# Latent attention on one core: the swapped rotary halves by transfers within SBUF in place of a second projection, and their sum on POOL

## The reference, cut to what matters

```python
kv_c = kv @ W_kvc                                   # 64 wide
q_c = q @ W_dq                                      # 96 wide
q_nope = (q_c @ W_uq).reshape(b, lq, H, HD)         # HD = 128
q_rope = (q_c @ W_qr).reshape(b, lq, H, R)          # R = 64
k_nope, v = kv_c @ W_uk, kv_c @ W_uv
k_rope = kv_c @ W_kr                                # 64, the same for all heads
q_rope, k_rope = _rope(q_rope), _rope(k_rope)       # [x1*cos - x2*sin, x1*sin + x2*cos]
scores = (q_nope . k_nope + q_rope . k_rope) / sqrt(HD + R)
out = softmax(where(good, scores, NEG)) @ v @ W_o
```

## Time and profile before

| | |
|---|---|
| median of 3 runs | 2310.97 us (2307.03 to 2313.88) |
| the profiled execution, its own time | 2306.32 us |
| its span, first to last instruction | 2304.5 us |
| busy share of the span | PE 89%, DVE 69%, ACT 54%, POOL 13% |
| mean granted clock of TensorE | 0.952 |
| the attention's four groups | some 80 us each, from 1200 to 1520 us of the span |

### The profile page before, as it was taken

The page is one execution under the profiler, slowest core; times in us unless marked ns, Lnnn a source line. Parts: engine busy times, 40 slices in busy tenths (PEclk is TensorE's granted clock), DMA queues, the critical chain, the costliest instruction groups (busy, mean ns, idle before and its releaser), DMA issues. The chain is left out here.

```text
span 2304.5 us, 46693 instructions
## 1 busy us (share of the span) xinstructions
PE 2055.2 (89%) x18816; PEld 1569.9 (68%) x18816; DVE 1600.1 (69%) x2975; ACT 1238.0 (54%) x2456; POOL 302.9 (13%) x307
## 2 busy tenths in 40 slices
PE   7978989899899898888889998979889779999996
PEld 4654458677555787566656666768656658999996
DVE  5756657677465897888857877857566676766763
ACT  2325664545476444555546547655478524665653
POOL 0010000011310000010000000000100113444432
PEclk9979999999999999999989999999899879999998
DMA  3020010100100002000020000010200035667663
GB/s 121 22 66 23 14 44 1 37 1 1 60 20 25 11 1 73 1 1 1 1 81 1 9 18 0 0 37 1 73 2 2 15 112 185 211 194 222 195 208 89
DMA packets 59688, 125.70 MB, mean 55 GB/s; under 512 B 12968, under 2 KB 42281, under 8 KB 59337
## 3 DMA queue, kind: packets, MB, share of 16 engines
q1 hardware_dynamic: 50666, 110.96, 14.2%
q0 software_dynamic: 8832, 12.06, 2.5%
HBM read 108.79 MB, written 15.80 MB: 54 GB/s over the span
## 5 line engine op out<-in xcount | busy, mean ns | idle before, releaser
L268 PE MATMUL ps<-ffn_xh,ffn_wh 128*128 128x256 f32 x644 | 184.1, 286 | 1.5 <-DVE ffn_xl L4388 1.5
L268 PE MATMUL ps<-ffn_xh,ffn_wl 128*128 128x256 f32 x644 | 182.2, 283 | 0.0
L268 PE MATMUL ps<-ffn_xl,ffn_wh 128*128 128x256 f32 x644 | 182.1, 283 | 0.0
L4383 DVE TENSOR_TENSOR ffn_wl<-ffn_fresh,ffn_wh 128x1792 fp32r<-128x1792 f32 x69 | 139.4, 2023 | 26.5 <-ACT ffn_wh L4263 26.5
L216 POOL TENSOR_TENSOR all_rstd<-all_mv,all_cst 128x4 f32<-128x4 f32 x40 | 8.5, 212 | 1060.8 <-DVE all_mv L194 1060.8
L1981 DVE SCALAR_TENSOR_TENSOR attn_xc<-attn_cx,all_w,attn_xc 128x512 f32<-128x512 f32 (+1 forms) x144 | 107.0, 749 | 40.2 <-ACT attn_xc L1832 36.8
L4263 ACT ACTIVATE ffn_wh<-ffn_fresh 128x1792 fp32r<-128x1792 f32 x69 | 116.9, 1695 | 14.6 <-DMA ffn_fresh<-in_l3f_w 14.6
L268 PEld LDWEIGHTS ps<-ffn_xh,ffn_wh 128*128 128x128 f32 x644 | 123.4, 192 | 1.7 <-DVE ffn_xl L4388 1.7
L268 PEld LDWEIGHTS ps<-ffn_xl,ffn_wh 128*128 128x128 f32 x644 | 123.5, 192 | 0.0
L268 PEld LDWEIGHTS ps<-ffn_xh,ffn_wl 128*128 128x128 f32 x644 | 123.4, 192 | 0.0
L3037 ACT ACTIVATE xattn_sc<-xattn_sc,xattn_mx 128x128 f32<-128x128 f32 x256 | 98.8, 391 | 17.7 <-DVE xattn_mx L3135 17.7
(11 more groups left out here) (486 smaller groups left out, 6065.6 us busy)
## 6 DMA issues: line engine op xcount, KB each, us to landing
ffn_fresh<-in_l3f_w SPq DMA_DIRECT2D x69, 896.0 KB, 4.9
all_w<-in_ctxT SPq DMA_DIRECT2D x12, 512.0 KB, 5.6
all_w<-in_ctx SPq DMA_DIRECT2D x8, 512.0 KB, 6.9
all_x<-in_x_rows SPq DMA_DIRECT2D x4, 512.0 KB, 7.4
all_x<-x_seq SPq DMA_DIRECT2D x4, 512.0 KB, 5.4
all_w<-in_l2x_o SPq DMA_DIRECT2D x1, 2048.0 KB, 9.4
xattn_ctxT<-in_ctxT SPq DMA_DIRECT2D x4, 512.0 KB, 3.8
all_w<-in_l2f_up SPq DMA_DIRECT2D x1, 2048.0 KB, 11.3
```

Source lines behind the costliest of these rows:

```text
L268: last = pe.matmul(out, a, b, start=start and n == 0, stop=stop and n == 2)
L4383: dve.tensor_tensor(wl[:, j % 2, piece(q)], fresh[:, piece(q)], wh[:, j % 2, piece(q)].bitcast(F32), ALU.subtract).then_inc(low_ready.sem, 1)
```

## The change

The second rotary product is gone, with its weights (`SWAP`, half of `wkr`) and their preparation. ACT now copies each rotary product out of PSUM into half 0 of a `rot` buffer (there are 5 in place of 3, `nB`). SP then issues four transfers, each of 32 partitions and 512 values (64 KB), that write half 1 of the buffer with the halves of each head swapped. DVE multiplies half 0 by cos and half 1 by sin, in place and from SBUF. POOL adds the two into `kR` or `qR`. The transfers of tile n wait until DVE has multiplied tile n - 3, since tiles three apart share a semaphore. `dist`, a scratch tile of the mask, moves from `rot` to `sc`. In the diff some long lines are cut where nothing changes.

```diff
-    LAT, ROPE, SWAP = range(3)
-    wh = k.sb("wh", [MQ, 3, PAIRS, P], F32R)
-    wkr = k.sb("wkr", [ML, 2, 2, MR])
+    LAT, ROPE = range(2)
+    nB = 5
+    wh = k.sb("wh", [MQ, 2, PAIRS, P], F32R)
+    wkr = k.sb("wkr", [ML, 2, MR])
...
-    rot = arena[:, 0:6 * T].rearrange("p (b m t l) -> p b m t l", b=3, m=2, t=TG)
+    rot = arena[:, 0:2 * nB * T].rearrange("p (b m t l) -> p b m t l", b=nB, m=2, t=TG)
-    dist = rot[:, 0, 0]
+    dist = sc[:, 0, 0]
...
                 act.activation(by_head(wh, ROPE), raw[:, :, :], ACT.Copy).then_inc(rounded.sem, 1)
-                act.activation(by_head(wh, SWAP)[:, :, 0:half], raw[:, :, half:MR], ACT.Copy).then_inc(rounded.sem, 1)
-                act.activation(by_head(wh, SWAP)[:, :, half:MR], raw[:, :, 0:half], ACT.Copy).then_inc(rounded.sem, 1)
...
-                dve.wait_ge(*rounded(0, 3))
-                for a, b in ((slice(0, half), slice(half, MR)), (slice(half, MR), slice(0, half))):
-                    dve.tensor_tensor(by_head(wl, SWAP)[:, :, a], raw[:, :, b], by_head(wh, SWAP)[:, :, a].bitcast(F32), ALU.subtract)
...
+            def swap(i, n):
+                sp.wait_ge(*rot_copied(i, n + 1))
+                if n >= 3:
+                    sp.wait_ge(*rot_ready(i, n - 2))
+                a = rot[:, n % nB].rearrange("p m t l -> p m (t l)")
+                for e in range(2):
+                    for h in range(2):
+                        into = slice(e * MR + h * half, e * MR + (h + 1) * half)
+                        from_ = slice(e * MR + (1 - h) * half, e * MR + (2 - h) * half)
+                        sp.dma_start(a[into, 1], a[from_, 0]).then_inc(swapped[n % 3].sem, 16)
+
             with sp.Fori(0, GROUPS - 1) as i:
+                for n in range(1 + PAIRS):
+                    swap(i, n)
                 sp.wait_ge(*ctx_used(i, 1))
                 sp.dma_start(ctxT[:, :, :], src[i + 1]).then_inc(ctx_loaded.sem, 16)
+            for n in range(1 + PAIRS):
+                swap(last_group, n)
...
             with pool.Fori(0, GROUPS) as i:
+                for n in range(1 + PAIRS):
+                    pool.wait_ge(*rot_ready(i, n + 1))
+                    a = rot[:, n % nB].rearrange("p m t l -> p m (t l)")
+                    pool.tensor_tensor(kR[:, :] if n == 0 else qR[:, n - 1, :], a[:, 0], a[:, 1], ALU.add).then_inc(rope_ready.sem, 1)
                 norm.pool(pool, i + 1)
...
-                for p in range(PAIRS):
-                    act.wait_ge(*lat_psum(i, p + 1))
-                    act.activation(qL[:, p, :], TB[(p + 1) % 2][:, :], ACT.Copy).then_inc(lat_ready.sem, 1)
+                for n in range(1 + PAIRS):
+                    act.wait_ge(*rot_psum(i, n + 1))
+                    if n >= nB:
+                        act.wait_ge(*rope_ready(i, n - nB + 1))
+                    act.activation(rot[:, n % nB, 0].rearrange("p t l -> p (t l)"), S[n % 4][:, :], ACT.Copy).then_inc(rot_copied.sem, 1)
+                    if n >= 1:
+                        act.wait_ge(*lat_psum(i, n))
+                        act.activation(qL[:, n - 1, :], TB[n % 2][:, :], ACT.Copy).then_inc(lat_ready.sem, 1)
...
                 for n in range(1 + PAIRS):
-                    dve.wait_ge(*rot_psum(i, n + 1))
...
-                    if n >= 1:
-                        add_halves(n - 1)
-                add_halves(PAIRS)
+                    dve.wait_ge(*swapped[n % 3](i, 64 * (n // 3 + 1)))
+                    for half_of, by in enumerate(("cos", "sin")):
+                        a = rot[:, n % nB, half_of]
+                        last = dve.tensor_tensor(a, a, k.c[by].unsqueeze(1).broadcast_to([P, TG, P]), ALU.mult)
+                    last.then_inc(rot_ready.sem, 1)
...
                 for n in range(1, 1 + PAIRS):
-                    if n >= 2:
-                        pe.wait_ge(*rot_ready(i, n - 1))
-                    for s in range(2):
-                        at = (slice(None), ROPE + s, n - 1, slice(None))
-                        last = three(pe, S[2 * s + n % 2][:, :], (wh, wl), (qh, ql), at, slice(None), True, True)
-                    last.then_inc(rot_psum.sem, 1)
+                    if n >= 4:
+                        pe.wait_ge(*rot_copied(i, n - 3))
+                    three(pe, S[n % 4][:, :], (wh, wl), (qh, ql), (slice(None), ROPE, n - 1, slice(None)), slice(None), True,
+                          True).then_inc(rot_psum.sem, 1)
...
-                pe.wait_ge(*rot_ready(i, 1 + PAIRS))
+                pe.wait_ge(*rot_copied(i, 1 + PAIRS))
                 scores(0)
```

More of the change, by code:

```diff
@@ L2854, in phase_xattn2 @@
     kvx = k.sb("kvx", [P, TG, ML])
-    rot = arena[:, 0:6 * T].rearrange("p (b m t l) -> p b m t l", b=3, m=2, t=TG)
-    pT = arena[:, 6 * T:10 * T].rearrange("p (b e n) -> p b e n", b=2, e=2)
+    rot = arena[:, 0:2 * nB * T].rearrange("p (b m t l) -> p b m t l", b=nB, m=2, t=TG)
+    pT = arena[:, 2 * nB * T:(2 * nB + 4) * T].rearrange("p (b e n) -> p b e n", b=2, e=2)
     qL = k.sb("qL", [P, PAIRS, T])
@@ L2966, in _ @@
                     dve.tensor_copy(wkv[:, :, e, :], v["kvc"])
-                    for s in range(2):
-                        dve.tensor_copy(wkr[:, s, e, :], v["kr"][:, s, :])
+                    dve.tensor_copy(wkr[:, e, :], v["kr"][:, 0, :])
                 dve.wait_ge(*small(0, 32))
@@ L2981, in phase_xattn2 @@
     rot_psum = Signal(k, "rot_psum", 1 + PAIRS)
+    rot_copied = Signal(k, "rot_copied", 1 + PAIRS)
+    swapped = [Signal(k, f"rot_swapped{b}", 64 * (1 + PAIRS) // 3) for b in range(3)]
     rot_ready = Signal(k, "rot_ready", 1 + PAIRS)
@@ L3104, in _ @@
                 scale_ternary()
-                def add_halves(n):
-                    dve.wait_ge(*rot_ready(i, n + 1))
-                    a = rot[:, n % 3].rearrange("p m t l -> p m (t l)")
-                    out = kR[:, :] if n == 0 else qR[:, n - 1, :]
-                    dve.tensor_tensor(out, a[:, 0], a[:, 1], ALU.add).then_inc(rope_ready.sem, 1)
-                for n in range(1 + PAIRS):
-                    dve.wait_ge(*rot_psum(i, n + 1))
-                    if n >= 3:
-                        dve.wait_ge(*rope_ready(i, n - 2))
-                    a, b = (S[2 * s + n % 2][:, :].rearrange("p (t l) -> p t l", t=TG) for s in range(2))
-                    dve.tensor_tensor(rot[:, n % 3, 0], a, k.c["cos"].unsqueeze(1).broadcast_to([P, TG, P]), ALU.mult)
-                    dve.tensor_tensor(rot[:, n % 3, 1], b, k.c["sin"].unsqueeze(1).broadcast_to([P, TG, P]),
-                                      ALU.mult).then_inc(rot_ready.sem, 1)
-                    if n >= 1:
-                        add_halves(n - 1)
-                add_halves(PAIRS)
+                for n in range(1 + PAIRS):
+                    dve.wait_ge(*swapped[n % 3](i, 64 * (n // 3 + 1)))
[3 more added lines that the diff above has]
+                    last.then_inc(rot_ready.sem, 1)
                 def scale(n, e):
@@ L3191, in _ @@
                 pe.wait_ge(*latent_ready(i, 1))
-                for s in range(2):
-                    last = pe.matmul(S[2 * s][:, :], wkr[:, s].rearrange("p e r -> p (e r)"), kL[0:ML, :], start=True, stop=True)
-                last.then_inc(rot_psum.sem, 1)
+                pe.matmul(S[0][:, :], wkr.rearrange("p e r -> p (e r)"), kL[0:ML, :], start=True, stop=True).then_inc(rot_psum.sem, 1)
                 pe.wait_ge(*rest_ready(i, 1))
                 for n in range(1, 1 + PAIRS):
-                    if n >= 2:
-                        pe.wait_ge(*rot_ready(i, n - 1))
-                    for s in range(2):
-                        at = (slice(None), ROPE + s, n - 1, slice(None))
-                        last = three(pe, S[2 * s + n % 2][:, :], (wh, wl), (qh, ql), at, slice(None), True, True)
-                    last.then_inc(rot_psum.sem, 1)
+                    if n >= 4:
+                        pe.wait_ge(*rot_copied(i, n - 3))
+                    three(pe, S[n % 4][:, :], (wh, wl), (qh, ql), (slice(None), ROPE, n - 1, slice(None)), slice(None), True,
+                          True).then_inc(rot_psum.sem, 1)
                     if n == 2:
```

2 lines of the change are left out of this document (1 added, 1 removed).

## The result

The changed kernel takes 2341.1 us in the median of four runs (2332.0 to 2347.15), the kernel before 2310.61 (2307.03 to 2313.88): a ratio of 1.0127, with a 95% interval of 1.0104 to 1.0149. It is 30.5 us slower. The forecast of "slower" holds, the forecast of 2325 us falls 16 us short, and the range ended 2 us too low.

A forecast was written before the change was run, and what follows sets the result against it. The prediction took DVE's first scale and scores(1)'s readiness for the second as the bound. Per group 1.7 + 2.2 = +3.9 us, four times 15.6, less 1.2, is +14.4: 2310.97 to 2325 us, range 2300 to 2339.

The forecast's parts named there:

- Which way, and the mechanism: Whole kernel: over 0.3% slower, 62%; rotary stage paced by SP and DVE-POOL turns, with the clock down, 42%.
- the price of an issue: SP's swaps in the rotary stage: 0.46 us per transfer, four a tile, so a tile every 2.0 us with waits.
- The turns of DVE and POOL: Rotary stage: DVE's multiplications and POOL's sum contend for SBUF, 2.40 us a tile times 0.84, 2.0 us.
- two stages of equal rate: Rotary stage: SP and DVE with POOL, linked by a wait three tiles back, run slower together: 2.15 us a tile.
- Landing: Swap transfers in the rotary stage: data lands 1.8 us after the issue, with 1.7 and 3.5 as the ends.
- ACT's copy: Rotary stage: ACT copies each tile out of PSUM in 0.60 us, with room since ACT sat idle.
- The clock: Idle PE halves the clock at scores(1), 3.6 us in place of 1.8, delaying the second scale: +2.2 us a group.
- The start of the main loop: End of the rotary stage: DVE free for its first scale at 1224.4 in place of 1222.72, +1.7 us a group.
- The preparation: Ahead of the groups: DVE's last two subtractions, which end the block, go: about -1.2 us, once.
- DVE and POOL strictly in turn: Rival in the rotary stage: full exclusion, 2.40 us a tile, 2333 us; part of the slower-chain rival, 20%.
- Landing after 3.5 us: Rival in the rotary stage: late swaps give 2.3 us a tile, 2337 us; part of the slower-chain rival, 20%.
- The warm clock: Rival at scores(1): the clock stays up and tiles take 2.0 us, +2.4 us in all, 2313 us; 20%.

The follow-up runs named there:

- experiment 1: Changed kernel with each tile swapped by two transfers of 64 partitions in place of four, computing other scores: 2324.03 us, 1.0072 of the kernel before.
- experiment 4: Changed kernel with one transfer moving the same 32 partitions of two tiles, 20 issues a group in place of 36: 2330.1 us, 1.0093 of the kernel before.
- experiment 7: Kernel before with only the sum of the halves moved to POOL, second projection kept, no transfers: 2309.38 us, ratio 1.0003.
- experiment 12: Changed kernel with two-tile transfers, the sum on DVE, and 6 and 8 idle PE products ahead of scores(0) and scores(1): 2330.42 us, 1.0097 of before.
- experiment 5: Changed kernel with the sum of the halves done by DVE again, four transfers a tile kept: 2337.42 us, 1.0125 of the kernel before.
- experiment 6: Changed kernel with two-tile transfers (20 issues a group) and the sum on DVE: 2322.59 us, 1.0056 of the kernel before.
- experiment 8: Changed kernel reordered: DVE multiplies straight from PSUM, SP swaps the sine products of two tiles per transfer, POOL subtracts, no ACT copies: 2302.0 us, 0.9960 of before.

## Why the prediction fell short

**Which way, and the mechanism: right.** SP's issues pace the stage, and the clock falls ahead of scores(1). PE starts the stage's last product 14.1 us after the subtraction (1209.62 less 1195.55) in place of 19.9 (1219.54 less 1199.67), and these 5.8 us buy nothing.

**The step that failed is the price of an issue**, "I take 0.46, 1.85 us for a tile, and 0.15 for the two waits ahead, so SP can deliver a tile every 2.0 us". It is 0.59 us long and comes every 0.64. The issues in my rows were of transfers with one end in DRAM. The trace of before had one issue with both ends in SBUF, the transfer of 512 KB whose landing I did use; its own length (ns) I did not look up:

```profile
L3009 SPq DMA_DIRECT2D all_x<-all_x x1: 527/527/527, 1360.2 to 1360.2; - x1
```

With that and four issues a tile the sum would have been 2.1 to 2.3 us, nearer but still short. What the 0.59 consists of no run here shows. The term, in a steady group: the pace of 2.56 in place of 2.15 makes 8 x 0.41 = 3.3 us, the first tile another 3 x 0.18 + 0.2 = 0.7. That is 4.0 a group, 16 us in four: all that was missing. What the clock took beyond the forecast (4 x 0.4) and what the preparation gave beyond it (1.1) nearly cancel, as said below.

**The turns of DVE and POOL: the size was off, and hidden.** I took 2.0 us, 2.40 with a factor of 0.84 from the earlier trace rows. Experiments 1 and 4 measured 2.27, which is 2.55 with a factor of 0.89; POOL's undisturbed sum, 1.12 by the line between two other sizes, is 1.26. That two stages of equal rate "do worse than either alone", which added 0.15, was not put to the test: the limits were unequal (2.56 and 2.27), the slower one alone set the pace, and in the changed kernel the two engines hardly meet. So the cost that the Trainium skill warns of ("SBUF — State Buffer", who interferes with whom) is real here and lay one step behind the bound; strict exclusion would give 2.55, and 2.27 was measured.

**Landing:** 1.8 expected, 2.0 measured in the median (1.9 to 2.9). The 2.0 us of fixed time in the Trainium skill, "DMA: Bandwidth & Descriptors", section "Anatomy of one DMA", which the prediction set beside its own, are given there for transfers that GpSimd issues; these are SP's. **ACT's copy:** 0.60, right; its waits for POOL do not reach SP.

**The clock:** +2.2 a group expected, measured 5.35 - 2.39 less the 0.37 that before loses to ACT, +2.6. **The start of the main loop:** +1.7 expected, 28.73 - 23.05 = +5.7 measured, by the failed step.

**The preparation:** -1.2 expected. From the start of the wide subtraction (1189.50 before, 1187.69 after) to that of `xattn_ql` it is 10.17 and 7.86 us, -2.3. The two subtractions are 1.2 of it. Nearly all the rest is the clock again, this time for the change: PE's product q_c ahead of the subtraction took 1.0 us less (before, then after).

```profile
1196.13 2.88 PE L260 MATMUL ps<-all_xnT,all_w 128*96 128x512 f32 x4
...
1193.01 1.88 PE L260 MATMUL ps<-all_xnT,all_w 128*96 128x512 f32 x4
```

The granted clock was 0.50 from 1196 to 1198 us before, and 1.00 from 1193 to 1195 us after. The kernels of the experiments have the same 1.88 us, and experiment 7, which keeps the preparation of before, has 2.87.

The sum with measured terms, 4 x 8.3 - 2.3 = +30.9, meets the +30.5 of the medians. The two profiled executions, from which the terms come, differ by less, 25.7 us. Their four groups, from the first subtraction to the start of the last scale, take 327.3 us in place of 293.5 (1522.85 less 1195.55, 1493.19 less 1199.67), +33.8 with the long first group, and the preparation -2.3. The other -5.8 us lie in code that the change leaves alone: 1.8 ahead of the wide subtraction and 4.0 behind the last scale. For the experiments the table and the same -2.3 give the medians to within 4.5 us. These are single executions set beside medians, so an agreement to 1 us is partly luck. Only experiment 12 is further off (13 us), whose profiled execution was much the longest.

**The rivals.** "DVE and POOL strictly in turn" had nearly the right time (2333) for a wrong reason, and experiment 5 rules it out as the cause: that 1.29 + 1.26 = 2.55 equals the distance seen is chance. Landing after 3.5 us did not happen. The warm clock did not either.

## What to carry to other kernels

Price an issue by an issue of the same kind, both ends considered, and count them: an engine that issues four transfers a tile is an engine with 2.56 us of work a tile. Find the one event behind which the group is rigid (here the second scale, 53.5 us ahead of the next group) and measure every variant to it; busy time saved ahead of it is worth nothing. If a transfer must stand in a chain, let the work that needs no transfer go first and fetch the swapped part for the last, cheap step: the same idea in that order turned 1.3% lost into 0.3 to 0.6% won.

## What the runs showed of the hardware

An issue within SBUF took 590 ns on SP with 64 KB, 590 with 128 KB on 64 partitions and 597 with 128 KB in two rows of 32 partitions: the price does not follow bytes. In the first groups one issue took 1.1 to 1.9 us (experiments 4 and 6, 1.4 in the changed kernel); why stays open. A product of two SBUF tiles on DVE that begins while POOL's sum is running goes from 0.69 to 1.75 us, and POOL's sum from 1.26 to 1.64; with the first input in PSUM (experiments 7 and 8) DVE's stays at 0.68 or 0.69. Two engines' transfers landed after 2.5 and 2.9 us in the median where one engine's took 2.3. With idle products in PE's gaps the granted clock stayed at 1.00 through all four groups, without them its mean was 0.90 and both scores ran at 0.50. An idle fp32 product of 128x512 takes 0.90 us, and a filler that does not fit its gap cost more (8 to 9 us) than the slow clock that it avoided.
